# Mamba layer of a decoder: B and C repeated over partitions by DMA, delta made tile by tile inside the scan

## The reference, cut to what matters

```python
xn = resid * rsqrt(mean(resid * resid) + eps) * norm_w
skip = einsum('bld,ed->ble', xn, skip_w)
x = silu(conv_b + causal_conv4(einsum('bld,ed->ble', xn, in_w), conv_w))
delta = softplus((x @ wd1.T) @ wd2.T + wd2_b)            # (b, l, e)
Bm, Cm = x @ wB.T, x @ wC.T                               # (b, l, 16)
A = -exp(A_log)
def step(h, (xt, dt, bt, ct)):
    h = exp(dt[:, :, None] * A) * h + (dt * xt)[:, :, None] * bt[:, None, :]
    return h, einsum('ben,bn->be', h, ct)
y = (scan(step) + W_D * x) * silu(skip)
out = resid + y @ out_w.T
```

## Time and profile before

| | us |
|---|---|
| median of 3 runs | 2859.72 |
| lowest, highest | 2859.01, 2860.47 |
| the profiled execution's own time | 2862.07 |
| its span, first to last instruction | 2860.3 |
| PE busy in the span | 2507.9 (88%) |
| DVE busy | 1402.8 (49%) |
| ACT busy | 897.6 (31%) |
| POOL busy | 557.9 (20%) |

### The profile page before, as it was taken

How to read it: one execution, slowest core, us unless ns; L and a number is a source line. 1 busy time by engine, 2 the same in 40 slices (tenths; PEclk the granted TensorE clock), 3 DMA queues, 4 the chain that set the end, 5 groups by cost and what they waited for, 6 DMA issues and landing times. The chain is left out here.

```text
span 2860.3 us, 32983 instructions
## 1 busy us (share of the span) xinstructions
PE 2507.9 (88%) x12313; PEld 1264.8 (44%) x12313; DVE 1402.8 (49%) x2005; ACT 897.6 (31%) x1869; POOL 557.9 (20%) x485
## 2 busy tenths in 40 slices
PE   7899999988999999896499899885997669999994
PEld 4544444434455555534245454353664323333331
DVE  5788888721578886721425512285444521111113
ACT  3644544402533334401112210085333112212210
POOL 0055555500000000001201100000000033343343
PEclk9899999999999999998799899997998879999997
DMA  2022222136535544308340000112000151560633
GB/s 86 25 72 82 75 85 79 66 87 241 187 112 185 175 139 120 126 15 243 117 156 0 2 39 3 50 41 88 1 1 1 53 233 52 232 265 23 261 101 116
DMA packets 94553, 288.64 MB, mean 101 GB/s; under 512 B 26924, under 2 KB 57288, under 8 KB 80188
## 3 DMA queue, kind: packets, MB, share of 16 engines
q1 hardware_dynamic: 59308, 158.34, 16.8%
q0 software_dynamic: 35104, 128.36, 12.6%
HBM read 449.40 MB, written 47.11 MB: 174 GB/s over the span
## 5 line engine op out<-in xcount | busy, mean ns | idle before, releaser
L684 POOL TENSOR_TENSOR x_rows<-ms_state,mb_C_everywhere 128x800 f32<-128x800 f32 x128 | 241.2, 1884 | 312.5 <-DVE ms_state L661 181.4
L694 PE MATMUL psum<-ms_context,mb_key_w 128*128 128x361 f32 x768 | 269.4, 487 | 23.0 <-ACT x_rows L604 9.6
L915 PE MATMUL psum<-at_Wv,at_context 128*128 128x512 f32 (+1 forms) x576 | 266.1, 601 | 0.0
L661 DVE TENSOR_TENSOR_SCAN ms_state<-ms_decay,psum 128x800 f32<-128x800 f32 x128 | 232.2, 1814 | 58.2 <-ACT ms_decay L611 41.3
L2639 PE MATMUL psum<-tf_W,tf_x_T 128*64 128x512 f32 x1024 | 232.3, 601 | 8.9 <-DMA tf_W<-in_L_W,tt_weight_row 8.9
L2661 PE MATMUL psum<-tf_W,tt_hidden 128*64 128x512 f32 x1024 | 227.2, 595 | 0.2 <-DMA tf_W<-in_L_W,tt_weight_row 0.2
L2694 ACT ACTIVATE tt_hidden<-psum,tf_b 128x64 f32<-128x64 f32 x512 | 111.7, 329 | 364.7 <-PE psum L2650 364.7
L694 PEld LDWEIGHTS psum<-ms_context,mb_key_w 128*128 128x128 f32 x768 | 136.3, 190 | 163.0 <-ACT x_rows L599 64.4
L2584 POOL DMA_INDIRECT tf_W<-in_L_W,tt_weight_row x128 | 126.9, 991 | 231.9 <-PE psum L2639 151.9
L1016 ACT ACTIVATE at_prob<-psum,at_neg_max 100x722 f32<-100x722 f32 x128 | 110.4, 863 | 145.9 <-DVE at_neg_max L1078 145.6
L1078 DVE TENSOR_REDUCE at_neg_max<-psum 100x1 f32<-100x722 f32 x128 | 115.6, 904 | 78.3 <-PE psum L936 77.9
(11 more groups left out here) (459 smaller groups left out, 3870.5 us busy)
## 6 DMA issues: line engine op xcount, KB each, us to landing
at_piece<-in_L_W_f POOLq DMA_DIRECT2D x24, 1024.0 KB, 6.3
keys_dram<-x_rows SPq DMA_DIRECT2D x128, 180.5 KB, 1.9
at_k_cols<-keys_dram SPq DMA_DIRECT2D x64, 361.0 KB, 3.2
sf_W<-in_L_W SPq DMA_DIRECT2D x16, 1024.0 KB, 7.5
tf_W<-in_L_W SPq DMA_DIRECT2D x8, 2048.0 KB, 26.0
ms_context<-in_ctxT SPq DMA_DIRECT2D x16, 541.5 KB, 4.4
at_context<-in_ctxT SPq DMA_DIRECT2D x8, 1083.0 KB, 5.1
ternary_dram<-at_piece_made POOLq DMA_DIRECT2D x14, 512.0 KB, 4.0
```

Source lines behind the costliest of these rows:

```text
L661: nc.vector.tensor_tensor_scan(state[:, n % RH, :], decay[:, g % RA, :, :].rearrange("p b l -> p (b l)"), drive[:, n % RD, :], 0.0, ALU.mu ...
L684: nc.gpsimd.tensor_tensor(seen[:, n % RH, :], state[:, n % RH, :], cC[:, n, :], ALU.mult).then_inc(weighed, 1)
L694: last = nc.tensor.matmul(side[:, 0:SH], lhsT=wk[:, k, e * P:(e + 1) * P], rhs=keys[:, h, k, :], start=(k == 0), stop=(k == KC - 1))
L915: last = nc.tensor.matmul(bank[0:rows_of(t), :], lhsT=ctxT[:, b % 2, k, t * P:t * P + rows_of(t)], rhs=wv[:, k, h * BANK:(h + 1) * BANK], ...
```

## The change

1. The norm of the preparation goes in two halves of four sequences, each as soon as its half of x is there.
2. In `mamba_inputs` only tile 0's delta is made. The products by ones, their copies and the split are gone. SP stores the 32 rows of B and C to a DRAM buffer, waits for it, and loads rows n = 0, 1, 2 of both back, each repeated over 128 partitions by the source's access pattern (410 KB a DMA). The context of the first key products is loaded in this block too.
3. In the scan's first tile SP issues rows n+3 ahead of its wait for key n; DVE and POOL wait for each row (`spread[n]`).
4. Delta of tile t+1 is made during tile t, in a buffer of two tiles: PE multiplies by wd2 in the side bank behind the sums of steps 1 and 2 (`DELTA_AT`), ACT copies it out with the bias (Identity), POOL clips behind its product 5, ACT does Abs, Exp and Ln in its steps 10, 11 and 12, and POOL adds behind its product 13 (`delta_ready`, for which ACT's next tile and DVE's next dx wait). Tile 7 has no successor, so this happens seven times.
5. ACT's and POOL's loops over tiles are written out instead of looped.

```diff
-            delta = sb2("delta", [P, KE, T])
+            delta = sb2("delta", [P, 2, T])
+            proj, wd2 = sb2("proj", [PROJ, T]), sb2("wd2", [PROJ, E_IN])
+            keys, ctx_loaded = sb2("context", [P, 2, KC, SH]), [c.sem(f"mb_context_loaded_{h}") for h in range(2)]
             bC = sb2("B_everywhere", [P, N_ST, T])
             cC = sb2("C_everywhere", [P, N_ST, T])
+            spread = [c.sem(f"mb_B_C_loaded_{n}") for n in range(N_ST)]
+            bc_dram = nc.dram_tensor("B_C_dram", (2 * N_ST, T), F32, kind="Internal").ap()
+            def spread_row(sp, n):
+                sp.dma_start(bC[:, n, :], bc_dram[n, :].partition_broadcast(P)).then_inc(spread[n], 16)
+                sp.dma_start(cC[:, n, :], bc_dram[N_ST + n, :].partition_broadcast(P)).then_inc(spread[n], 16)
...
-        squares, ms, rstd = sb("squares", [L, D]), sb("mean_square", [L, NB]), sb("rstd", [L, NB])
+        squares, ms, rstd = sb("squares", [L, 2, D]), sb("mean_square", [L, NB]), sb("rstd", [L, NB])
...
+            for h in range(2):
+                sp.dma_start(keys[:, h, :, :], dram["ctxT"][0, :, :, h * SH:(h + 1) * SH]).then_inc(ctx_loaded[h], 16)
+            for h in range(2):
+                sp.wait_ge(proj_ready, h + 1)
+                sp.dma_start(bc_dram[:, half(h)], proj[DR:PROJ, half(h)]).then_inc(bc_stored, 16)
+            sp.wait_ge(bc_stored, 32)
+            for n in range(AHEAD):
+                spread_row(sp, n)
...
-            for u, (e, h) in enumerate(tiles):
-                prod.wait_free(pe, len(tiles) + u)
-                nc.tensor.matmul(prod.bank(u)[:, 0:HALF], lhsT=wd2[:, e * P:(e + 1) * P],
+            for h in range(2):
+                prod.wait_free(pe, len(tiles) + h)
+                nc.tensor.matmul(prod.bank(h)[:, 0:HALF], lhsT=wd2[:, 0:P],
                                  rhs=proj[:, half(h)], start=True, stop=True).then_inc(prod.filled, 1)
-            def spread_row(ring, u, row, h):
-                ring.wait_free(pe, u)
-                ones_at = pick[:, row:row + 1].broadcast_to([PROJ, P])
-                nc.tensor.matmul(ring.bank(u)[:, 0:HALF], lhsT=ones_at, rhs=high[:, half(h)], start=True, stop=False)
-                nc.tensor.matmul(ring.bank(u)[:, 0:HALF], lhsT=ones_at, rhs=low[:, half(h)], start=False, stop=True).then_inc(ring.filled, 1)
-            pe.wait_ge(parts_ready, 2)
-            for u, (n, h) in enumerate(spread):
-                if n == N_ST - KE + POS_X and h == 0:
-                    pe.wait_ge(delta_done, KE)
-                spread_row(bsp, u, DR + n, h)
-                spread_row(csp, u, DR + N_ST + n, h)
...
+            for h in range(2):
+                act.wait_ge(positive_done, h + 1)
+                nc.scalar.activation(delta[:, 0, half(h)], prod.bank(h)[:, 0:HALF], ACT.Abs,
+                                     bias=vec[:, 0, DC + 1:DC + 2]).then_inc(sized, 1)
+            act.wait_ge(sized, 2)
+            nc.scalar.activation(delta[:, 0, :], delta[:, 0, :], ACT.Exp, scale=-1.0).then_inc(exped, 1)
+            act.wait_ge(exped, 1)
+            nc.scalar.activation(delta[:, 0, :], delta[:, 0, :], ACT.Ln, bias=1.0).then_inc(logged, 1)
...
-            pool.wait_ge(ms_ready, 1)
-            nc.gpsimd.tensor_tensor(rstd[:, :], rstd[:, :], power[:, :], ALU.pow).then_inc(rstd_ready, 1)
+            for z in range(2):
+                pool.wait_ge(ms_ready, z + 1)
+                part = slice(z * HB, (z + 1) * HB)
+                nc.gpsimd.tensor_tensor(rstd[:, part], rstd[:, part], power[:, part], ALU.pow).then_inc(rstd_ready, 1)
...
+            for z in range(2):
+                dve.wait_ge(squared, (z + 1) * HB)
+                part = slice(z * HB, (z + 1) * HB)
+                nc.vector.tensor_scalar(rstd[:, part], ms[:, part], 1.0 / D, EPS, ALU.mult, ALU.add).then_inc(ms_ready, 1)
+                dve.wait_ge(rstd_ready, z + 1)
+                for b in range(z * HB, (z + 1) * HB):
+                    nc.vector.tensor_scalar(xn[:, b, :], c.x[:, b, :], rstd[:, b:b + 1], None, ALU.mult).then_inc(normed, 1)
...
-            nc.vector.tensor_copy(pick[:, :], c.ident[0:PROJ, 0:PROJ]).then_inc(parts_ready, 1)
-            dve.wait_ge(proj_ready, 2)
-            nc.vector.tensor_copy(high[:, :], proj[:, :]).then_inc(split, 1)
-            dve.wait_ge(split, 1)
-            nc.vector.tensor_tensor(low[:, :], proj[:, :], high[:, :].bitcast(F32), ALU.subtract).then_inc(parts_ready, 1)
-            for u, (e, h) in enumerate(tiles):
-                prod.wait_full(dve, len(tiles) + u)
-                nc.vector.tensor_scalar(positive(e)[:, half(h)], prod.bank(u)[:, 0:HALF], vec[:, e, DC + 1:DC + 2],
+            for h in range(2):
+                prod.wait_full(dve, len(tiles) + h)
+                nc.vector.tensor_scalar(positive[:, half(h)], prod.bank(h)[:, 0:HALF], vec[:, 0, DC + 1:DC + 2],
                                         0.0, ALU.add, ALU.max).then_inc(positive_done, 1)
-            bsp.grant(dve)
-            for u, (n, h) in enumerate(spread):
-                bsp.wait_full(dve, u)
-                nc.vector.tensor_copy(bC[:, n, half(h)], bsp.bank(u)[:, 0:HALF]).then_inc(bsp.done(u), 1)
-                if h == 1 and n < KE:
-                    dve.wait_ge(logged, n + 1)
-                    nc.vector.tensor_tensor(delta[:, n, :], delta[:, n, :], positive(n), ALU.add).then_inc(delta_done, 1)
-def mamba_scan(c, xc, vec, delta, bC, cC, negA, wk, wk_loaded, k_dram):
+            dve.wait_ge(positive_done, 2)
+            dve.wait_ge(logged, 1)
+            nc.vector.tensor_tensor(delta[:, 0, :], delta[:, 0, :], positive[:, :], ALU.add).then_inc(delta_done, 1)
...
+        DELTA_AT, CLIP_AT, CURVE_AT, ADD_AT = [1, 2], 5, 10, 13
+        def side_order(last):
+            order = []
+            for n in range(N_ST):
+                order.append(("key", n))
+                if n in GATE_AT:
+                    order.append(("gate", GATE_AT.index(n)))
+                if n in DELTA_AT and not last:
+                    order.append(("delta", DELTA_AT.index(n)))
+            return order
+        SIDE = len(side_order(False))
+        at_side = lambda t, last, kind, u: t * SIDE + side_order(last).index((kind, u))
...
-            def store(t, more):
+            def store(t, first=False, last=False):
                 for u in range(N_ST):
                     h, e = divmod(u, KI)
-                    sp.wait_ge(side_taken, t * SIDE + side_of_key(u) + 2)
+                    if first and u + AHEAD < N_ST:
+                        spread_row(sp, u + AHEAD)
+                    sp.wait_ge(side_taken, at_side(t, last, "key", u) + 2)
                     sp.dma_start(k_dram[bass.ds(t, 1), :, e, h * SH:(h + 1) * SH].rearrange("a p s -> (a p) s"),
                                  made[:, u % 2, :]).then_inc(key_stored[u % 2], 16)
-                    if more and e == KI - 1:
+                    if not last and e == KI - 1:
                         load(t + 1, h)
-                if more:
+                if not last:
                     load_skip(t + 1)
             for r in range(2):
                 sp.sem_inc(key_stored[r], 16)
-            load(0, 0)
             load_skip(0)
-            load(0, 1)
-            with sp.Fori(0, KE - 1) as t:
-                store(t, True)
-            store(KE - 1, False)
+            store(0, first=True)
+            with sp.Fori(0, KE - 2) as t:
+                store(t + 1)
+            store(KE - 1, last=True)
...
+            def take_delta(t, j, h):
+                act.wait_ge(side_filled, at_side(t, False, "delta", h) + 1)
+                nc.scalar.activation(delta[:, 1 - j, half(h)], side[:, 0:HALF], ACT.Identity,
+                                     bias=vec[:, bass.ds(t + 1, 1), DC + 1:DC + 2].rearrange("p a v -> p (a v)")).then_inc(side_taken, 1)
+            def curve(t, j, z):
+                act.wait_ge(clipped, t + 1)
+                act.wait_ge(curved, t * 3 + z + 1)
+                at = delta[:, 1 - j, :]
+                if z == 0:
+                    ins = nc.scalar.activation(at, at, ACT.Abs)
+                elif z == 1:
+                    ins = nc.scalar.activation(at, at, ACT.Exp, scale=-1.0)
+                else:
+                    ins = nc.scalar.activation(at, at, ACT.Ln, bias=1.0)
+                ins.then_inc(curved, 1)
...
+                if not first:
+                    act.wait_ge(delta_ready, t)
                 for n in range(N_ST):
                     g = j * N_ST + n
                     act.wait_ge(scanned, i * per + g + 1 + (not first and g < per % RA))
-                    nc.scalar.activation(decay[:, g % RA, :, 1:], seqs(tile_of(delta, i, j))[:, :, 1:], ACT.Exp,
+                    nc.scalar.activation(decay[:, g % RA, :, 1:], seqs(delta[:, j, :])[:, :, 1:], ACT.Exp,
                                          scale=tile_of(negA, i, j)[:, n:n + 1]).then_inc(decayed, 1)
                     if n == SCALE:
```

(91 more changed lines are left out.)

42 lines of the change are left out of this document (14 added, 28 removed).

## The result

The kernel after takes 2864.52 us (median of 20 runs, 2855.28 to 2868.66) where the kernel before, run beside it, takes 2860.51 (20 runs, 2854.88 to 2865.58). The ratio is 1.0014, with an interval of 1.0007 to 1.0020: it is slower by 2 to 6 us, where 8.2 us less was forecast. The time lies inside the range stated for 8 cases in 10 (2842 to 2867), but outside the prediction's own range of this case (2845 to 2861), and the sign is the wrong one. Its profiled span is 2862.3 us, against 2860.3.

A forecast was written before the change was run, and what follows sets the result against it. PE was taken to bound the scan. Start -41.5, DMA-fed tile +1.0, early context -0.5, delta products +20.6, Ln +12.2 gave -8.2 us: 2859.7 to 2851.5 us, with 2842 to 2867 for 8 in 10.

The forecast's parts named there:

- What bounds the kernel: Scan: PE, busy 52.31 of 55.12 us a tile; work on it or between side-bank copies lengthens a tile.
- Second half of the preparation: Preparation, projection to first dx: only tile 0's delta remains, 7.7 us instead of 47.2, gaining 39.5.
- the earlier start: Start of the preparation: the norm in two halves gains 2.0 us, between 1 and 2.5.
- Ln: Seven scan tiles: Ln on ACT with two table loads costs PE 1.74 us a tile, 12.2 in all.
- The third rival: Scan: Ln and Exp share one table set, costing PE 0.5 us instead of 1.74; 2842.5 us; 7%.
- Delta's products on PE: Seven scan tiles: two halves of 1.47 us each on PE, 2.94 a tile, 20.6 us in all, nothing hiding them.
- Clip and sum on POOL: Seven scan tiles: clip about 1.9 us, sum 1.88, both hidden; at most 1 us a tile if not.
- The second rival: Scan: extra ACT or POOL work delays the next tile's first decay; 1.5 us a tile, 2862 us; 17%.
- the first tile fed by DMA: Scan tile 0: rows of B and C arriving by DMA cost 1.0 us, bounds 0 and 13.
- The rival that stood for it: Scan tile 0: rows come too slowly, binding below about 260 GB/s; 2874 us at 180; 12%.
- Sum: Whole kernel: all terms together give -8.2 us, 2859.7 to 2851.5 us, 0.29% faster.
- the sign of failure: Scan tile 0: the forecast fails if this tile takes over 67 us; under 61 was expected.

The follow-up runs named there:

- experiment 4: Kernel after, with each tile's Ln in the scan replaced by a second Exp, so no table changes for it; 2852.5 us, ratio 0.9968.
- experiment 1: Kernel after, with rows of B and C issued six steps ahead instead of three; 2852.08 us, ratio 0.9973.
- Experiment 7: Kernel after, but B and C spread in the preparation by PE's products as before, so only delta moves to the scan; 2876.73 us, ratio 1.0057.
- Experiment 3: Kernel after, lead still three, but in tile 0 DVE issues scan n ahead of the wait for row n+1 and drive n+1; 2853.24 us (one run).
- experiment 2: Kernel after, with rows of B and C issued four steps ahead instead of three; 2853.87 us (one run).
- experiment 6: Kernel after, but delta of all tiles made in the preparation and twelve rows issued there instead of three; 2835.64 us, ratio 0.9911.
- experiment 5: Kernel after, but delta of all eight tiles made in the preparation; rows by DMA, lead three; 2848.34 us, ratio 0.9956.

## Why the prediction was wrong, by its own steps

**What bounds the kernel: right.** PE set the pace of the tiles from tile 2 on, and what was put on it or between two copies of the side bank lengthened the tile.

**Second half of the preparation, and the earlier start: right.** The first dx comes at 87.57 (87.5 forecast). The product of in_w starts 3.3 us earlier (22.43 against 25.75), not 2.0, and the stretch up to the projection gives 1.3 back.

**Ln: right.** 1.74 us were counted on PE; key 11 starts 4.59 behind key 10 (204.60 to 209.19) instead of 2.86, which is 1.73, and experiment 4 takes away just that. There are two loads a tile, and each is followed at once: the load starts at 204.35, the Ln at 205.65, the next load at 206.53, the decay at 207.83. The Trainium skill (ScalarE: Activation LUTs, "What ACT_TABLE_LOAD costs") adds 1.38 us of drain to each load; the trace again disagrees, with 0.02 between the end of a load and its function. Its sentence that ln and exp share a set ("Table sets: the hidden batching unit") isn't borne out as this kernel was compiled: the decay behind the Ln has its own load. The third rival is out (its time comes to 2842.8 by its own terms, not 2842.5).

**Delta's products on PE: right in kind, the size a little low.** A half takes 173.01 - 171.38 = 1.63 us, not 1.47: ACT's Identity starts 0.98 behind the product (0.83 forecast) and PE follows it 0.06 behind. With the Ln that makes 2 x 1.63 + 1.73 = 4.99 of the 5.09 us by which a tile grew, against 4.68 forecast. A tenth is left without a name. Over the seven tiles the whole comes to 2.9 us more than forecast.

**Clip and sum on POOL: right.** The clip takes 2.22 us (1.9 taken, bounds 0 and 3.8), the sum 1.88. In tile 1 the sum ends at 216.04, and dx follows at 218.05 with nothing waiting. The second rival shows only at the end of tile 0, where the sum was late because its tile was (154.32, and ACT idle for 5.83).

**The step that failed: the first tile fed by DMA.** It counted 1.0 us with bounds 0 and 13; measured against a run in which the rows come in time (experiment 1) it is 69.27 - 58.97 = 10.3 us in tile 0 and 1.1 in tile 1. Experiment 7, which has no rows to fetch, takes 58.91 for tile 0. With 54.02 + 4.68 + 1.0 - 0.5 = 59.2 the forecast of tile 0 without this fault was good: experiment 1 has 58.97. The prediction had the loop before it, with 10 to 11 us from the copy of key u-1, and then said that "PE's sum for row u+3 comes four steps of 2.86 after that of key u-1". That is the wrong consumer of the data. The first to wait for row u+3 is DVE, for drive u+3; it does so ahead of scan u+2, and sum u+2 needs that scan. So PE has three steps, 8.6 us, and not four, 11.4, in which to cover a chain that was put at 10 to 11 us and measures 11.2. Where a gate or a delta half falls in between, it is covered (sums 4 to 7 and 9 to 11). Where none does, it is not: sum 8 waits 2.67. The Ln covers only a part: sum 12 still waits 1.10, and sum 13 waits 1.75, since the copy of key 10 that releases its row itself stands behind the Ln's two loads (142.54). Experiment 3 shows it directly, since undoing only this order takes these waits away and brings tile 0 to 59.47, with the head start named there; experiments 1 and 2 show it by the lead. That the 10.3 us lie inside the bounds of 0 and 13 is luck: the 13 was worked out from a rate, not from this loop, and the prediction's own range let the term go only to 4.

How the 11.4 us reach the end can be read from PE, beside experiment 1. Its waits in the rows above are 2.67, 1.10, 1.75 and 2.27, less the 0.99 behind the Silu that they swallow: 6.8 us. The rest is the clock. The granted clock falls behind the wait of 2.67, to the lower level (1.2 GHz), and the gate half that follows takes 4.60 (130.34), where experiment 1 has this on the upper one (2.4 GHz):

```profile
127.37 2.91 PE L746 MATMUL psum<-x_cols,x_rows 128*64 128x400 f32 x16
```

That is 1.69; key 14, behind the wait of 2.27, takes 3.75 instead of 2.09, 1.66 more; and the first steps, which stay on the lower level longer than in experiment 1, add 1.0 (sum 0 takes 1.61 and key 1 3.93, against 0.90 and 3.65). That makes 11.2 of 11.4, and a good third of it is the slower clock, not waiting. The last piece isn't a cost of the late rows. It comes ahead of all of them; experiment 4, with the same lead, doesn't have it (0.90 and 3.74), while experiment 2 does (1.61 and 3.98). So it goes with the execution, and some 10.4 us are left for the late rows.

**The rival that stood for it** (rows too slow in tile 0, 12%) had the place right and the mechanism wrong. It expected a limit in GB/s, read as 243 from a load that repeats one row; but the queue in experiment 6 moves repeated rows at 407 GB/s when it is kept full. In tile 0 of the kernel after it moved 217 with a share of 0.69, so part of the time it had nothing to move. The rate isn't without weight: 217 at 0.69 comes to some 315 GB/s at a full share, an estimate, against 395 where rows go alone (407 at a share of 1.03), and the 1.0 MB of a step's rows and key store then take 3.2 us, more than PE's 2.86. But experiment 1 moves the same bytes, and the lead alone takes the waits away. The Trainium skill (DMA: Bandwidth & Descriptors, "Anatomy of one DMA — SWDGE (gpsimd) path") fits a DMA issued by GpSimd with 2.0 us fixed and its bytes over 436 GB/s. These are issued by SP; if the fit is taken for the two of a row all the same, it gives 3.9 us, an estimate from the page. The trace has 5.55 from the first issue (119.18) to the drive (124.73), with a key's store in front.

**Sum.** The end of the scan was forecast 8.2 us earlier and came 5.5 later. Of the difference of 13.7, tile 0 makes 10.1, tile 1 1.4 (of which 0.3 is its share of the per-tile error), tiles 2 to 6 2.0, the rest 0.2. The prediction had itself named the sign of failure, tile 0 over 67 us. What the chances lacked was a case of latency rather than rate. The second rival (the sum on POOL late) took part only as a consequence: of the wait of 2.27 at key 14, part is ACT's idle 5.83 for that sum.

## What to carry to other kernels

For data that is fetched just in time, work out the whole loop from the event that releases the issue to that same event some steps later, and take as consumer the first instruction in any queue that waits for it, together with all that stands behind it there, not the one that uses the result. If the loop over the lead comes out near the pace of the bounding engine, lengthen the lead: here three rows more were worth 12 us on the median and 10.7 at the end of the scan. And price a move in both places: delta took 18.7 us in the preparation and 35.6 in the scan, since there it stood on the engine that bounds it.

## What was not expected of the hardware

- A repeat of one DRAM row over 128 partitions runs at 407 GB/s when several are queued (experiment 6), and a pair of them, issued singly behind a key's store, is there some 5.5 us after its first issue (119.18 to 124.73).
- PE's granted clock fell behind one wait of 2.67 us: it is 1.00 in the window 128 to 130, 0.64 in 130 to 132 and 0.51 in 132 to 134. The waits of 1.66 at an Ln left it at 1.00: tiles 2 to 6 each have one, and a mean of 1.00. The length of a single wait doesn't settle it. It fell behind one of 2.31 in experiment 4 (0.72 in the window 167 to 170) and one of 2.65 in experiment 5 (0.72 in 128 to 134), but not behind one of 2.62 in experiment 2 (1.00 in 160 to 164), nor one of 3.13 in experiment 5 (1.00 in 166 to 176).
- An elementwise maximum with a constant takes 2.22 us on POOL for 128x800, longer than the product of two such tensors (1.87 to 1.94 in the scan).
